# The output stage is spread over the attention steps, and the search for the maxima runs nine groups ahead instead of eleven

## What is computed

```python
xn = layernorm(x)                                  # per token, eps 1e-5
qkv = (xn @ w_qkv).reshape(b, s, 3, 16, 16)        # 16 heads of 16
q = q / 4
scores = where(causal, einsum('bqhd,bkhd->bhqk', q, k), -1e10)
s = einsum('bhqk,bkhd->bqhd', softmax(scores), v).reshape(b, s, 256) @ w_out
y = xn
for i in range(6):                                 # feed-forward blocks, hidden 1024
    y = gelu(y @ W1[i].T + B1[i]) @ W2[i].T + B2[i] + y
    if i < 5: y = layernorm(y) * LN_G[i] + LN_B[i]
out = x + s * silu(y)
```

## Time and profile before

| | us |
|---|---|
| median of 3 runs (lowest, highest) | 1761.65 (1760.46, 1762.91) |
| profiled execution, its own time | 1765.19 |
| its span, first to last instruction | 1763.5 |
| busy: PE, DVE, ACT, POOL | 1656.3, 1149.4, 870.6, 305.8 |
| mean granted TensorE clock | 0.972 |

### The profile page before, as it was taken

One profiled execution on the slowest core, in us unless ns is written; L12 is line 12 of the kernel. 1 busy time (PEld: TensorE's weight loads), 2 busy tenths in 40 slices (PEclk: granted clock), 3 DMA queues, 4 the chain that ended last, 5 costly groups with the idle time before them and its releaser, 6 DMA issues. The chain is left out here.

```text
span 1763.5 us, 29499 instructions
## 1 busy us (share of the span) xinstructions
PE 1656.3 (94%) x11216; PEld 1345.9 (76%) x11216; DVE 1149.4 (65%) x2924; ACT 870.6 (49%) x1220; POOL 305.8 (17%) x290
## 2 busy tenths in 40 slices
PE   6989999999999999999999999999998998899656
PEld 5879888888888888898888888889986443334246
DVE  7736776787877777778776777765554554454045
ACT  3444443444444444444443444344444998899522
POOL 1031111111111111111111111111102232223113
PEclk9989999999999999999999999999998999999868
DMA  8859334251020201202021020220302455533324
GB/s 279 300 179 210 84 86 92 83 121 50 16 50 13 43 13 26 39 13 49 14 43 23 10 46 13 37 76 1 62 1 60 115 155 128 147 101 94 97 94 157
DMA packets 73033, 141.88 MB, mean 80 GB/s; under 512 B 9984, under 2 KB 49408, under 8 KB 66112
## 3 DMA queue, kind: packets, MB, share of 16 engines
q1 hardware_dynamic: 72896, 140.05, 30.0%
HBM read 109.34 MB, written 55.84 MB: 94 GB/s over the span
## 5 line engine op out<-in xcount | busy, mean ns | idle before, releaser
L616 ACT ACTIVATE m_hid<-m_h_ps,m_b1s 128x512 f32<-128x512 f32 x384 | 264.7, 689 | 718.5 <-PE m_h_ps L714 696.4
L677 DVE TENSOR_TENSOR m_hidl<-m_hid,m_hidh 128x512 fp32r<-128x512 f32 x384 | 279.9, 729 | 269.4 <-ACT m_hidh L619 268.7
L867 ACT ACTIVATE a_prob<-a_st_ps 128x1024 f32<-128x1024 f32 x288 | 277.6, 1022 | 28.3 <-PE a_st_ps L905 22.9
L727 PE MATMUL m_y_ps<-shared,m_hidh 128*128 128x256 f32 x1536 | 284.5, 283 | 0.0
L714 PE MATMUL m_h_ps<-m_xth,shared 128*128 128x512 f32 x768 | 276.2, 401 | 6.3 <-issue 4.0
L592 POOL TENSOR_TENSOR xres<-xres,m_b2s 128x1024 f32<-128x1024 f32 x48 | 132.7, 2766 | 756.2 <-DVE xres L633 756.2
L619 ACT ACTIVATE m_hidh<-m_h_ps,m_b1s 128x512 fp32r<-128x512 f32 x384 | 260.7, 679 | 0.0
L727 PEld LDWEIGHTS m_y_ps<-shared,m_hidh 128*128 128x128 f32 x1536 | 248.1, 189 | 14.8
L727 PE MATMUL m_y_ps<-w2h,m_hidh 128*128 128x256 f32 x768 | 216.7, 282 | 0.0
L727 PE MATMUL m_y_ps<-shared,m_hidl 128*128 128x256 f32 x768 | 215.8, 281 | 0.0
L727 PE MATMUL m_y_ps<-w2l,m_hidh 128*128 128x256 f32 x768 | 214.0, 279 | 0.0
(11 more groups left out here) (114 smaller groups left out, 2713.9 us busy)
## 6 DMA issues: line engine op xcount, KB each, us to landing
shared<-q_stacks SPq DMA_DIRECT2D x32, 400.0 KB
shared<-k_stacks SPq DMA_DIRECT2D x32, 400.0 KB
q_stacks<-q_parts SPq DMA_DIRECT2D x96, 128.0 KB
k_stacks<-k_parts SPq DMA_DIRECT2D x96, 128.0 KB
mk<-k_stacks SPq DMA_DIRECT2D x32, 384.0 KB, 10.7
q_parts<-mq SPq DMA_DIRECT2D x16, 512.0 KB, 4.2
k_parts<-mk SPq DMA_DIRECT2D x16, 512.0 KB, 3.6
mq<-q_stacks SPq DMA_DIRECT2D x21, 384.0 KB, 4.9
```

The costliest lines, as they stand in the source:

```text
L616: nc.scalar.activation(hid[n % 2][:], h_ps[n % 2][:], ACT.Gelu, bias=b1s[i % 2][:, k:k + 1])
L677: nc.vector.tensor_tensor(hidl[n % 4][:], hid[n % 2][:], hidh[n % 4][:].bitcast(F32), ALU.subtract).then_inc(low_done, 1)
L727: m = nc.tensor.matmul(y_ps[:, j, :], h[n % 4][:, j * P:(j + 1) * P], w[par][:, k, :], start=(k == 0 and j % 2 == 0 and h is hidh and w is ...
L867: nc.scalar.activation(to, scores, ACT.Exp).then_inc(exp_done, 1)
```

## The change

There are two parts.

1. `combine` is gone. What it did is now in `attend`. After each half of a group, SP moves the 16 rows of each head from `oout` to a tile `num` that has the layout which the projection needs (SBUF to SBUF, 4 DMAs), and the row of denominators to DRAM (4 DMAs). After each second group, per half, the denominators of 8 heads are loaded as a 128 x 32 tile (`gather`), inverted on DVE (`invert`), stored (`keep`), loaded again, each spread over the 16 rows of its head (`spread`, 8 DMAs), multiplied in (`divide`, DVE), and split (`high` on POOL, `low` on DVE). The table `DELAYS` says how many steps after the copy of `o_ps` each stage stands. After the fourth group of a batch, the 8 tiles of that batch are projected (`project_tile`, six matmuls each, with `s_ps` of the search as their PSUM), mixed with the gate on DVE (`mix`), summed on POOL and stored. The transposes are gone. The gate is computed as y * (1 + tanh(y / 2)) / 2 instead of silu: for seven of the eight groups of tokens in `mlp`'s last block, with one activation and one DVE product each; for the last group in `attend`, at step 18.
2. `AHEAD` is 9. In `mlp` lie 188 visits, in `attend` 148, spread over 124 steps, so that 24 steps hold two. On PE a step is now: scores 0, visit, scores 1, values, a second visit if the step has one, and a tile's projection if one is due. The load for the search (four DMAs) goes at a step 1, 4 or 7 of a group.

The core of the diff (renamings of views and declarations are left out):

```diff
-AHEAD = 11
+AHEAD = 9
...
+            def half_tanh(t):
+                act.wait_ge(b2_added, t + 1)
+                xx = xres[:, TILES * (t % GROUPS):TILES * (t % GROUPS) + TILES, :]
+                nc.scalar.activation(keep["tanh"], xx, ACT.Tanh, scale=0.5).then_inc(tanh_done, 1)
...
+                    if k == 5:
+                        dve.wait_ge(tanh_done, t - LAST + 1)
+                        nc.vector.scalar_tensor_tensor(xx, keep["tanh"], 1.0, xx, ALU.add, ALU.mult).then_inc(gated, 1)
...
+DELAYS = {"move": 1, "gather": 3, "invert": 5, "keep": 5, "spread": 7, "divide": 9, "high": 9, "low": 11}
+LAST_DELAYS = {"move": 1, "gather": 2, "invert": 3, "keep": 3, "spread": 4, "divide": 5, "high": 5, "low": 6}
...
+def part_copied_at(n, half):
+
+    return NS * n + LAST_STEP[half] + LATE
+
...
+def part_schedule():
+
+    stages, tiles = {}, {}
+    for n in range(N_GROUPS):
+        last = n == N_GROUPS - 1
+        for half in range(2):
+            at = part_copied_at(n, half)
+            for stage, delay in (LAST_DELAYS if last else DELAYS).items():
+                if n % 2 or stage == "move":
+                    stages.setdefault(at + delay, []).append((n, half, stage))
+            if n % HG == HG - 1:
+                for j in range(TILES):
+                    tiles.setdefault(at + (7 + j if last else 13 + 3 * half + 2 * j), []).append(QT * (n // HG) + TILES * half + j)
+    return stages, tiles
...
-        AT.setdefault(NS * (N_GROUPS - 2) * (v - VISITS[0]) // len(VISITS), []).append(v)
+        AT.setdefault((NS * (N_GROUPS - 2) - 2) * (v - VISITS[0]) // len(VISITS), []).append(v)
...
+            def move(n, half):
+                sp.wait_ge(o_copied, 2 * n + half + 1)
+                if n >= 4 and n % 2 == 0:
+                    sp.wait_ge(normed, n - 3 + half)
                 for j in range(HG):
-                    sp.dma_start(od[hg, j, :, SEQ * bt:SEQ * (bt + 1)],
-                                 oout[n % 2][2 * HD * j:2 * HD * j + HD + 1, :]).then_inc(o_stored[n % 2], 16)
-
+                    to = slice(HG * HD * (n % 2) + HD * j, HG * HD * (n % 2) + HD * (j + 1))
+                    sp.dma_start(num[n // 2 % 2][half][to, :], oout[half][2 * HD * j:2 * HD * j + HD, :]).then_inc(moved[half], 16)
+                    row = 2 * HD * j + HD
+                    sp.dma_start(scratch["den"][n // 2, half, HG * (n % 2) + j:HG * (n % 2) + j + 1, :], oout[half][row:row + 1, :]).then_inc(den_stored[half], 16)
...
+            def gather(n, half):
+                sp.wait_ge(den_stored[half], 16 * HG * (n + 1))
+                if n >= 2:
+                    sp.wait_ge(inv_stored[half], 16 * (n // 2))
+                sp.dma_start(flat[half][:], scratch["den"][n // 2, half].rearrange("h (c t) -> (h c) t", t=FLAT)).then_inc(flat_loaded[half], 16)
...
+            def keep_inverse(n, half):
+                sp.wait_ge(inverted, n // 2 * 2 + half + 1)
+                sp.dma_start(scratch["inv"][n // 2, half].rearrange("h (c t) -> (h c) t", t=FLAT), flat[half][:]).then_inc(inv_stored[half], 16)
+
+            def spread(n, half):
+                sp.wait_ge(inv_stored[half], 16 * (n // 2 + 1))
+                if n >= 2:
+                    sp.wait_ge(divided, n // 2 * 2 + half - 1)
+                for h in range(2 * HG):
+                    sp.dma_start(den[half][HD * h:HD * (h + 1), :], scratch["inv"][n // 2, half, h:h + 1, :].broadcast_to([HD, BANK])).then_inc(inv_loaded[half], 16)
...
-                        search.load(sp, m + 2)
+                        searched.append(m + 2)
+                if step in (1, FOURS + 1, NS - 2) and searched:
+                    search.load(sp, searched.pop(0))
...
-                    store_o(n - 1)
...
+                for n, half, stage in STAGES_AT.get(at, ()):
+                    if stage == "high":
+                        pool.wait_ge(divided, n // 2 * 2 + half + 1)
+                        if n >= HG:
+                            pool.wait_ge(proj_done, QT * (n // HG - 1) + TILES * (half + 1))
+                        nc.gpsimd.tensor_copy(onh[half][:, n % HG // 2, :], num[n // 2 % 2][half][:]).then_inc(high_done, 1)
+                for i in TILES_AT.get(at - 1, ()):
+                    c = i % TILE_BUFS
+                    pool.wait_ge(mixed, i + 1)
+                    pool.wait_ge(x_loaded[c], 16 * (i // TILE_BUFS + 1))
+                    nc.gpsimd.tensor_tensor(res[c][:], res[c][:], xt[c][:], ALU.add).then_inc(added, 1)
...
                 dve.wait_ge(av_done, NS * n + LAST_STEP[half] + 1)
-                if n >= 2:
-                    dve.wait_ge(o_stored[n % 2], 16 * OUT_DMAS * (n // 2))
-                nc.vector.tensor_copy(oout[n % 2][:, BANK * half:BANK * (half + 1)], o_ps[half][:]).then_inc(o_copied, 1)
...
+                if n:
+                    dve.wait_ge(moved[half], 16 * HG * n)
+                    dve.wait_ge(den_stored[half], 16 * HG * n)
+                nc.vector.tensor_copy(oout[half][:], o_ps[half][:]).then_inc(o_copied, 1)
...
+                if stage == "invert":
+                    dve.wait_ge(flat_loaded[half], 16 * nth)
+                    nc.vector.reciprocal(flat[half][:], flat[half][:]).then_inc(inverted, 1)
+                elif stage == "divide":
+                    dve.wait_ge(moved[half], 16 * HG * (n + 1))
+                    dve.wait_ge(inv_loaded[half], 16 * 2 * HG * nth)
+                    nc.vector.tensor_tensor(values[:], values[:], den[half][:], ALU.mult).then_inc(divided, 1)
+                elif stage == "low":
+                    fh = n % HG // 2
+                    dve.wait_ge(high_done, count)
+                    nc.vector.tensor_tensor(onl[half][:, fh, :], values[:], onh[half][:, fh, :].bitcast(F32), ALU.subtract).then_inc(normed, 1)
...
+                dve.wait_ge(proj_done, i + 1)
+                if i >= TILE_BUFS:
+                    dve.wait_ge(stored[c], 16 * (i // TILE_BUFS))
+                if i == N_TILES - TILES:
+                    dve.wait_ge(gated, 1)
+                nc.vector.scalar_tensor_tensor(res[c][:], s_ps[:, i % 2, 0:DIM], 0.5, xres[:, i, :], ALU.mult, ALU.mult).then_inc(mixed, 1)
...
+            for at in range(END):
                 for v in AT.get(at, ()):
                     search.dve_visit(dve, s_ps, v)
...
+                for half in range(2):
+                    n, left = divmod(at - LATE - LAST_STEP[half], NS)
+                    if left == 0 and 0 <= n < N_GROUPS:
+                        copy_o(n, half)
+                for n, half, stage in STAGES_AT.get(at, ()):
+                    normalise(n, half, stage)
+                for i in TILES_AT.get(at, ()):
+                    mix(i)
...
+            def project_tile(i, seen):
+                half, j = i % QT // TILES, i % TILES
+                if j == 0:
+                pe.wait_ge(search.maxed, 2 * seen)
+                if i >= 2:
+                    pe.wait_ge(mixed, i - 1)
+                for c in range(HALVES):
+                    for t, w in ((onh, woh), (onh, wol), (onl, woh)):
+                        m = nc.tensor.matmul(s_ps[:, i % 2, 0:DIM], t[half][:, c, P * j:P * (j + 1)], w[:, c, :],
+                                             start=(c == 0 and t is onh and w is woh), stop=(c == HALVES - 1 and t is onl))
+                m.then_inc(proj_done, 1)
...
+            for at in range(END):
                 n, step = divmod(at, NS)
                 if at < ALL:
                     scores(n, step, 0)
+                visits = AT.get(at, ())
+                for v in visits[0:1]:
+                    if projected:
+                        pe.wait_ge(mixed, projected)
+                    search.pe_visit(pe, s_ps, v, False)
+                if at < ALL:
+                    scores(n, step, 1)
                 if 0 <= at - LATE < ALL:
                     values(at - LATE)
-                if at < ALL:
-                    scores(n, step, 1)
-                for v in AT.get(at, ()):
+                for v in visits[1:]:
                     search.pe_visit(pe, s_ps, v, False)
```

More of the change, by code:

```diff
@@ L867, in _ @@
                     nc.scalar.activation(to, scores, ACT.Exp).then_inc(exp_done, 1)
+                if at == GATE_AT:
+                    nc.scalar.activation(tanh[:], xres[:, N_TILES - TILES:N_TILES, :], ACT.Tanh, scale=0.5).then_inc(tanh_done, 1)
         @block.vector
@@ L1102, in gated_block @@
+                seen = visits[-1] + 1 if visits else seen
+                for i in TILES_AT.get(at, ()):
+                    project_tile(i, seen)
+                    projected = i + 1
 def gated_block(nc, x, wqkv, wout, w1t, b1, w2t, b2, ln_g, ln_b, out):
```

280 lines of the change are left out of this document (100 added, 180 removed).

## The result

The changed kernel takes **1796.04 us** (median of 4 runs, 1788.09 to 1800.40) against 1761.82 us of before on the same chip: a ratio of 1.0181, 95% interval 1.0161 to 1.0201. It is slower by 34 us. The profiled execution has a span of 1796.5 us, 33.0 us above that of before.

What follows compares the result with a forecast made beforehand. It took PE to bound mlp, PE and ACT at one pace to bound attend; -19 + 109 - 76 = +14 us on the 1761.65 median gave 1775 us, range 1725 to 1808 (forecast alone 1766 to 1790).

Steps and rivals of the forecast that it cites:

- Term 1: In mlp: 42 visits leave, full pieces saving PE 0.47 us each, added tanh and products hidden; -19 us.
- Term 2: In attend: steps priced by round trips through the one PSUM tile s_ps; 361 us against 307.
- While a step holds one use, the trip hides in its 1.98 us: In attend: steps with at most one visit or tile stay at 1.98 us; 103 steps, 204 us.
- the path is not the sum of PE's work: In attend: s_ps must be read by DVE before the next write, so round trips are priced; a visit 1.84 us.
- Term 3: In attend: DVE's product waits for late spread inverses, 41 us, plus 14 us of lowered clock.
- The clock's 14: In attend: 3.5 us of lost time at lowered clock behind each of four larger waits; 14 us, bounds 0 and 30.
- a queue served in order: On SP's queue in attend: small stores land only after large loads ahead, about 20.5 us after the stacks' issue.
- Term 4: After the last exponentials: a 27 us end replaces 103.5 us; -76 us.
- A: Rival, attend: transfers aren't late, waits and clock cost under 41 us instead of 55; faster, 1720 us; chance 0.20.
- B: Rival, attend: s_ps trips overlap more, saving 24 us in 41 crowded steps; faster, 1724 us; chance 0.12.
- C: Rival, attend: crowded steps leave PE idle and the clock falls, losing 20 us; slower still, 1795 us; chance 0.12.

Runs made afterwards that it cites:

- part2_only: Kernel before with AHEAD 9, visits over 124 steps, the new PE order and visits ahead of copies on DVE; last stage stays: 1763.95 us, ratio 1.0012.
- nochain11: Changed kernel without the denominators' gather, reciprocal, store and spread (product takes the values twice), and with eleven groups searched ahead instead of nine: 1701.15 us.
- no_chain: Changed kernel without the denominators' gather, reciprocal, store and spread; the product takes the values twice: 1720.86 us.
- act_loads: Changed kernel with the large loads of attend (stacks, search, values) issued from ACT's queue, small transfers still from SP's: 1849.29 us.

## Why the prediction was right or wrong

The direction was right and the time inside the wide range, but outside the forecast's own 1766 to 1790; the likeliest value, 1775, was 21 us short of the median. By the two spans the sum should have been +33.0 where I had +14. Measured by the experiments, the four terms are -26.9 + 67.0 + 64.9 - 72.0 = +33.0, against -19 + 54 + 55 - 76. The terms of attend were too small by 13.0 and 9.9 us, the end by 4.0, and the gain in mlp by 7.9; that two errors partly cancel is luck.

**Term 1, -19.** Mlp gave 26.9 us, 0.64 for each of 42 visits, where I had PE's 0.47 of the earlier trace rows. With part2_only 26.3 and nochain11 28.4 it is no scatter. Of the further 0.17, some 0.08 is PE's waits for DVE at the visits, which fell from 5.2 to 1.8 us up to 1322; the rest was not isolated. That tanh and gating are hidden was right: part2_only, without them, starts attend 0.6 us later, not sooner.

**Term 2, 361 against 307.** Without the chain attend takes 372.8. **The step that failed** is "While a step holds one use, the trip hides in its 1.98 us". The starts of the exponentials give each step's length. A second visit stands behind its step's scores, so its cost shows in the step after it.

| steps, mean us (count) | before | part2_only | no_chain | I had |
|---|---|---|---|---|
| no visit, no tile | 2.22 (38) | 1.97 (20) | 1.95 (16) | 1.98 |
| one visit | 2.09 (106) | 2.14 (100) | 2.24 (84) | 1.98 |
| tile alone | | | 2.98 (4) | 1.98 |
| after two visits | | 3.50 (24) | 3.31 (20) | 3.52 |
| visit and tile | | | 3.53 (16) | 3.30 |
| tile, after two visits | | | 4.69 (4) | 5.06 |

The price of a second use came out: crowded steps take over 3 us. With packing I had 155 us for 41 of them; 40 took 141. The steps with at most one use took 231 us in no_chain, 2.22 each, where I had 206. The 1.98 us came from one quiet place; the mean step of the kernel before is 305.8 / 144 = 2.12, waits for stacks and slow first steps included, and I set a sum on 1.98 against a measured 307. Nor is PE's work free beside the trip, as "the path is not the sum of PE's work" has it: of the 67.0 us PE is busy for 48.8 (337.8 against 289.1). I had also put no clock cost into this term. By the intervals of the granted clock, PE is busy 35.7 us at half speed in no_chain and 17.7 before; half of the difference, 9 us, is the most that this can have cost.

**Term 3, 41 of waits and 14 of clock.** By groups my waits for the third, fifth, seventh, ninth and eleventh were 8, 14, 4, 11 and 4 us; DVE waited 10.7, 13.5, 5.5, 11.2 and 7.2 there. I had none for the last groups, and these waited 13 more (3.5 in the thirteenth, 9.9 in the last two): 61.3 in all. I had also thought of the product alone: 12.2 of the 61.3 us stand at the reciprocal. So the waits were the part that I undersized, by 20 us. The clock's 14 was about right: PE is busy 68.9 us at half speed in the change and 35.7 without the chain, which costs at most half of the difference, 17 us. As the waits and this together cost 64.9 us and not 61 + 17, some of each lay under other work. The reason given for the lateness, a queue served in order, was not the main one (act_loads); that its sizes were nearly right is luck, as they came from the landing of the earlier trace rows, which holds all the bytes whatever the reason.

**Term 4, -76.** -72.0. The transfers' issue was the term that I undersized: SP takes 0.51 and 0.43 us for a head's two transfers and 0.44 for a spread, not 0.3. The end without the chain is 20.1 us, so the chain's last passage is 11.1.

**The rivals.** A's condition, waits and clock under 41 us, was not met: 65. B, overlapping trips, fell with no_chain, where attend is above my 361 us and not 24 below, and with nochain11. C had the right time, 1795, and half the right reason: the clock did fall, behind waits for transfers above all, and not from crowding alone (no_chain 37 us of half clock, part2_only 40, the change 96). Rows that I had named in advance came as said: an end under 35 us, waits of up to 13 us in the named groups, crowded steps over 3 us, and 26 to 35 us for five of the six groups where tiles are projected. The sixth, the fifteenth, took 20.5, groups without a tile but with a long wait took up to 37 (the fifth), and the last 21.4 where I had 18 to 20. Mlp's last matmul ended at 1321.8 rather than near 1330.

## What to carry to other kernels

Before work of a drained last stage is put between the steps of a busy one, write down its chain of small transfers, and count both what each hop stands behind and how long the issuing engine is held: its in-order waits pass a late hop on to transfers that have nothing to do with it. Fewer transfers for the same bytes, with the consumer several steps later, with eleven groups searched ahead as before, turned +34 us into -38. Moving visits into the stage with the one PSUM tile did not pay: 0.68 us left the earlier stage for each visit and 1.14 came back, since steps with two uses took 3.3 to 3.5 us against some 2.1. And where a sum is built on a step's length, take the mean of the stage and not one quiet place of it.

## What the hardware showed that I had not expected

A transfer of 16 KB took 12.5 us to land from a queue that had issued nothing for 6.7 us, while 3.1 MB were under way from another engine's queue (15.4 us in the same queue, and 1.44 with no large load under way). And the granted clock stayed at its lower level, 1.2 GHz, well after PE had work again: in the third group PE stood for 10.7 us, and the clock was at half speed for 10 us more with PE busy for 8.97 of them. In attend the time at half clock was 13 us where no wait of ACT for scores was over 2.4 us (nochain11), 37 where none was over 3.2 (no_chain), and 96 where they reached 13.1.
